# The column copies of a token mix: three engines share what GpSimd did for the most part

## The reference, cut to what matters

```
v = fno_layer(tokens_norm, value_w, value_skip_w, value_skip_b, (H, W))
dprod = softmax(einsum('bhtd,bhsd->bhts', qf, kf) / scale)
attn = einsum('bhts,bhsd->bhtd', dprod, vf)
attn = fno_layer(attn, proj_w, proj_skip_w, proj_skip_b, (H, W))
attn = instance_norm(attn + tokens, attn_norm_g, attn_norm_b)
m = instance_norm(attn, norm2_g, norm2_b)
m = fno_layer(m, mixer_w1, ..., norm=(mixer_norm_g1, mixer_norm_b1), act=gelu)
```

## Time and profile before

| | |
|---|---|
| median of 3 runs | 540.05 us (538.45 to 540.66) |
| profiled execution | 538.36 us |
| its span | 536.6 us |
| TensorE busy, matmuls | 378.2 us (70%) |
| VectorE busy | 380.9 us (71%) |
| ScalarE busy | 264.1 us (49%) |
| GpSimd busy | 280.3 us (52%) |
| GpSimd's column copies, L587 | 24, 30.1 us, 1296 ns each |

### The profile page before, as it was taken

How to read it: one execution, slowest core, us unless ns; L and a number is a source line. 1 busy time by engine, 2 the same in 40 slices (tenths; PEclk the granted TensorE clock), 3 DMA queues, 4 the chain that set the end, 5 groups by cost and what they waited for, 6 DMA issues and landing times.

```text
span 536.6 us, 8617 instructions
## 1 busy us (share of the span) xinstructions
PE 378.2 (70%) x3153; PEld 294.4 (55%) x3153; DVE 380.9 (71%) x982; ACT 264.1 (49%) x523; POOL 280.3 (52%) x294
## 2 busy tenths in 40 slices
PE   0489999974556699999994094766566556799590
PEld 0488996944111599988983083433333225466490
DVE  4999424264957776279997948677777656999791
ACT  1467742330210387346550131688888976599000
POOL 0587998300002496899898156766666069700000
PEclk9998999788687799779997587599999996899796
DMA  8969970499920200001665000000000000000299
GB/s 234 291 159 247 285 206 1 98 220 256 421 112 0 60 2 2 0 1 55 183 174 160 1 0 1 0 1 2 0 2 0 1 1 0 1 0 1 76 285 267
DMA packets 61082, 51.03 MB, mean 95 GB/s; under 512 B 4896, under 2 KB 54480, under 8 KB 60016
## 3 DMA queue, kind: packets, MB, share of 16 engines
q1 hardware_dynamic: 61040, 50.48, 33.4%
HBM read 30.45 MB, written 16.88 MB: 88 GB/s over the span
## 4 chain that ended last, share of the span: by engine, by line
DVE 41%; PE 25%; POOL 13%; ACT 6%; issue 5%; DMA 4%; SPq 3%; DVEq 0%
PE PS L628 23%; DVE PS L1430 7%; DVE BIG L1226 5%; DVE SML L1128 5%; POOL BIG L614 3%; DVE BIG L1398 3%; POOL BIG L545 3%; DMA BIG<-BIG 3%; POOL BIG L609 2%; PE PS L632 2%; DVE SML L1412 2%; DVE BIG L1315 2%; DVE BIG L1481 2%; SPq L502 2%; POOL BIG L561 2%
## 5 line engine op out<-in xcount | busy, mean ns | idle before, releaser
L628 PE MATMUL PS<-CST,BIG 128*128 128x122 f32 (+7 forms) x996 | 134.0, 330 | 30.8 <-POOL BIG L545 22.3
L628 PEld LDWEIGHTS PS<-CST,BIG 128*128 128x128 f32 (+1 forms) x996 | 119.1, 208 | 48.6 <-issue 36.0
L632 PE MATMUL PS<-CST,BIG 128*128 128x128 f32 (+1 forms) x326 | 53.7, 312 | 73.2 <-ACT SML L382 26.8
L632 PEld LDWEIGHTS PS<-CST,BIG 128*128 128x128 f32 (+1 forms) x326 | 43.4, 188 | 94.8 <-issue 59.9
L628 PE MATMUL PS<-BIG 128*32 128x32 f32 (+2 forms) x1216 | 67.7, 391 | 18.0 <-DVE BIG L1226 13.7
L587 POOL COPY BIG<-BIG 128x512 f32<-128x512 f32 x24 | 30.1, 1296 | 80.5 <-DVE BIG L1226 72.4
L628 PEld LDWEIGHTS PS<-BIG 128*32 128x32 f32 (+1 forms) x1216 | 50.8, 229 | 33.7 <-issue 17.1
L1128 DVE BATCH_NORM_STATS2 SML<-BIG 128x6 f32<-128x128 f32 x256 | 58.8, 301 | 9.1 <-DMA BIG<-in_x 7.8
L609 POOL TENSOR_TENSOR BIG<-BIG,SML 128x512 f32<-128x512 f32 x32 | 33.3, 1041 | 47.2 <-DVE SML L1150 30.5
L545 POOL TENSOR_SCALAR BIG<-BIG,SML 128x128 f32<-128x128 f32 x72 | 44.0, 676 | 24.5 <-DVE SML L1150 24.5
L628 PE MATMUL PS<-BIG,SML 128*128 128x256 f32 (+3 forms) x214 | 49.8, 471 | 5.8 <-ACT BIG L1076 5.8
(11 more groups left out here) (207 smaller groups left out, 588.7 us busy)
## 6 DMA issues: line engine op xcount, KB each, us to landing
xn_rows<-BIG SPq DMA_DIRECT2D x8, 1024.0 KB, 9.5
BIG<-xn_rows SPq DMA_DIRECT2D x8, 1024.0 KB, 23.9
BIG<-in_x SPq DMA_DIRECT2D x32, 256.0 KB, 2.9
out_x<-BIG SPq DMA_DIRECT2D x32, 256.0 KB, 3.7
BIG<-wy_rows SPq DMA_DIRECT2D x16, 192.0 KB, 6.2
BIG<-BIG SPq DMA_DIRECT2D x16, 192.0 KB, 11.5
BIG<-in_L_conv_mixer_w SPq DMA_DIRECT2D x2, 544.0 KB, 6.1
CST<-in_const SPq DMA_DIRECT2D x1, 579.5 KB, 8.9
```

The source lines that it names most:

```text
L628: return pe.matmul(o, l, rhs, start=start, stop=stop, **k)
L632: return pe.matmul(o, i, ident[0:n, 0:n], is_transpose=True, start=True, stop=True)
```

## The change

GpSimd keeps the even groups. VectorE takes groups 1, 5, 9, ..., 29 and ScalarE keeps 3, 7, ..., 31. VectorE's copies stand at four places of its block: group 1 ahead of the wait for `p_ma`, group 5 after L1284, groups 9 and 13 after L1287, groups 17, 21, 25 and 29 after L1297. There is one new semaphore, `x_mix_dve`.

```
             for g in range(32):
-                if g % MIX_ACT != MIX_ACT - 1:
+                if g % 2 == 0:
                     if g >= MIX_RING:
                         pool.wait_ge(S("mix_filled"), g + 1 - MIX_RING)
...
-                if g % MIX_ACT == MIX_ACT - 1:
-                    pe.wait_ge(S("x_mix_act"), (g + 1) // MIX_ACT)
+                if g % 2 == 0:
+                    pe.wait_ge(S("x_mix_pool"), g // 2 + 1)
                 else:
-                    pe.wait_ge(S("x_mix_pool"), g + 1 - (g + 1) // MIX_ACT)
+                    pe.wait_ge(S("x_mix_act" if g % 4 == 3 else "x_mix_dve"), g // 4 + 1)
...
+            def mix_columns(*groups):
+
+                for g in groups:
+                    if g >= MIX_RING:
+                        dve.wait_ge(S("mix_filled"), g + 1 - MIX_RING)
+                    dve.tensor_copy(x_mix[:, g % MIX_RING], columns(g)).then_inc(S("x_mix_dve"), 1)
...
             dve.wait_ge(S("ma"), 1)
 
+            dve.wait_ge(S("xt_in"), 16 * XC)
+            mix_columns(1)
             dve.wait_ge(S("p_ma"), 1)
...
             link(TS(y_m, y_m, s("al"), None, ALU.mult))
+            mix_columns(5)
             dve.wait_ge(S("kap_filled"), 1)
             dve.tensor_copy(kap, PS[:, 3, 0:NT]).then_inc(S("kap"), 1)
             link(TT(s("x0"), s("sm"), s("sm"), ALU.mult))
+            mix_columns(9, 13)
             dve.wait_ge(S("p_z1"), 1)
...
             TS(z3_1[:, :, 0, :], z3_1[:, :, 2, :], -1.0, None, ALU.mult).then_inc(S("z3_1"), 1)
+            mix_columns(17, 21, 25, 29)
```

## The result

The changed kernel takes 544.39 us (median of 6 runs, 541.33 to 548.77) against 538.32 (median of 6, 533.78 to 540.66): **1.0168 times the kernel before, 95% interval 1.0121 to 1.0215**. All ratios here are those on record, taken over the fast executions of both kernels; they are not the quotient of the two medians, which is 1.0113 in this case. In a second series the ratio was 1.0125 (1.0079 to 1.0172). The kernel is slower, as forecast, and its time is inside the range. The profiled execution, 548.77 us with a span of 547.0, is the slowest of its six.

A forecast was written before the change was run, and what follows sets the result against it. TensorE was taken to bound the mix, not the copies. Standstills of 2.7 and 3.3 us less 0.6 regained make 5.4, with 1.7 for the clock 7.1; on the median of 540.05 this gives 547.1 us, range 542.4 to 551.

The forecast's parts named there:

- The two late copies: VectorE's copies of groups 5 and 17 come late in the mix; TensorE stands still 2.7 and 3.3 us.
- The sum: For the mix: standstills 2.7 and 3.3, less 0.6 regained, 5.4 us; with 1.7 for the clock, 7.1.
- The third term: Standstill before group 17: its copy comes 6.0 us after group 13's end, TensorE wants it after 2.7; 3.3 us.
- The one fall: TensorE's clock halves after the second standstill, 3.4 us of work losing 1.7 us; ends 0 and 3.4.
- The copy's price: One VectorE column copy, every element read with a stride, takes 0.65 us; ends 0.43 and 1.1.
- The copy of group 1: VectorE's copy ahead of the wait for p_ma delays the start by some 0.1 us; ends 0 to 0.6.
- The meetings: GpSimd's copies of 6 and 8 hold up VectorE before group 5, that of 20 before 17; 1.0 us each.
- Group 11: Its 0.6 us lateness, from ScalarE's late copy, is regained if zw comes before ScalarE needs it.
- Group 9's copy follows at once, 3 us ahead of its use: VectorE's copy of group 9, right behind that of 5, was to be in time by 3 us.
- TensorE bounds this stage, not the copies: In the token mix GpSimd's 24 copies arrive in time, up to five groups ahead; TensorE sets the pace.
- The relief of the lock: Rival: fewer GpSimd copies free VectorE's chain, group 11's gap closes, nothing new is late; 539.4 us; 6%.
- The row of GpSimd operations that would starve a VectorE copy: Rival: each late VectorE copy loses another 1 us behind GpSimd's, both standstills cost clock; 10.8 us more, 550.9; 14%.

The follow-up runs named there:

- e6: The changed kernel run again without edits, in a second series; 1.0125 times the kernel before, profiled mix 40.89 us.
- e1: Changed kernel with only VectorE's copy of group 17 moved early, between the request for root r1 and its taking; 1.0087 times the kernel before.
- e2: Changed kernel with only VectorE's copy of group 5 moved early, between the second and third products for zw; 1.0064 times the kernel before.
- e5: e3 with VectorE's copy of 9 also ahead of the y_m scaling and that of 21 ahead of the z3_1 addition; 1.0001 times the kernel before.
- e4: Changed kernel with the copies of groups 5 and 17 given back to GpSimd, which makes 18; 1.0039 times the kernel before.
- e3: Changed kernel with VectorE's copies of groups 5 and 17 both moved early; 1.0023 times the kernel before.
- e9: Kernel before the change, plus 14 matrix products of constants on TensorE ahead of its wait for the scaled identity; 1.0052 times the kernel before.
- e10: e5 plus 14 matrix products of constants on TensorE ahead of the mix; 1.0033 times the kernel before.
- e8: Changed kernel with GpSimd holding its copies of groups 8 and 20 until VectorE's of 5 and 17 are done; 1.0097 times the kernel before.

## Why the prediction was right

**The two late copies.** Right in place, order and cause. Forecast 2.7 and 3.3 us; measured idle 2.79 and 2.83 (2.49 and 2.85 in e6), and by the starts of groups 3.0 each. e1 and e2 take them away one by one, e5 both with what they had hidden.

**The sum.** Forecast 2.7 - 0.6 + 3.3 + 1.7 = 7.1 for the mix with one fall; measured 6.75. In the medians it is 6.1 us. The third term was 0.3 too large; most of it is L1294 (now L1305), which took 1.95 with its meeting where I had 1.2 + 1.0. The time forecast, 547.1 us, is 2.7 above the measured median of 544.39: 1.0 of it is the sum, and 1.7 is the median of the kernel before, 540.05 over three executions and 538.32 over six.

**The one fall.** Here luck helped. The fall was a choice between none and two; the profile of the changed kernel has one, of 1.70 us, and that of the same kernel in e6 none, with a mix 5.1 us longer than before against the 5.4 forecast without a fall. The medians' 6.1 lies between the two.

**The copy's price.** 0.65 taken, 0.73 to 0.75 measured, 0.80 right after a wait. That lies between L1374 (0.43) and L1277 (1.10), which fits a charge for the stride; no run here changes the stride alone. By the two results a cycle that the Trainium skill gives for a float32 copy within SBUF ("VectorE: DVE Perf Modes", section "Mode 2×_2P — use both read ports for one tensor") the copy would take the 0.43 of L1374, an estimate; the trace doesn't bear that out for this copy.

**The copy of group 1.** The request ends at 179.14 and ScalarE takes the root at 179.18, when its own copy is done too; from VectorE's L1266 (before: L1259) to the first group it is 5.64 us, 5.45 before. Forecast some 0.1, measured 0.2.

**The meetings.** Their number was right (two before group 5, one before 17) and their price near: 1.0 us each in the forecast, 0.8, 0.9 and 0.7 measured (L1290, L1291 and L1305 less what they take alone). Their partners were not. I had GpSimd's copy of 6 hold up L1280 (now L1289). In fact that copy was ready at 185.24, during L1288, and L1289 still went ahead of it in its own 1.15 us; the operations held up were L1290 and L1291. That didn't move the sum.

**Group 11** was regained, as forecast: no idle stands there. The changed kernel alone doesn't show the reason, since its standstill before group 5 gives ScalarE time as well; in e5, which has no such standstill, group 11 is in time too.

**What was wrong, though the sum didn't show it.** Two sentences hold only under a condition that the prediction doesn't name. "Group 9's copy follows at once, 3 us ahead of its use" and "Groups 21, 25 and 29 follow back to back or wait for a slot, in time" are true only while TensorE stands still before 5 and 17. e2 to e4 show 9 late by 1.3 to 2.3 us, and e1, e3 and e4 show 21 late by 0.2 to 1.0, once it doesn't. And "TensorE bounds this stage, not the copies" holds only at the clock of the earlier trace rows: e9 shows the copies binding once the first groups run at 1.00.

**The rivals.** The relief of the lock was real and small: `zw` came 8.3 us after the mix's start (189.69), not 10.0 (190.85). TensorE doesn't wait for `zw` itself, and the 0.7 us at group 11 is all that could come of it; the copies of 5 and 17 were late all the same. The row of GpSimd operations that would starve a VectorE copy did not occur; the longest copy of the changed kernel is 0.80 us, and those of e5 and e10, at most 1.57, were held up by one operation. The Trainium skill ("SBUF — State Buffer", section "Who interferes with whom") says that the engine that issues first has the shared ports for its whole instruction while the other is blocked. e8 agrees with it: with GpSimd's copy of 8 away, L1291's 1.54 us became 0.68.

What stays open: in which executions the clock falls behind a standstill. Of the timed executions only the mean clock is known, and one profile was taken of each kernel (two of the changed one). Open too is where most of e9's time goes.

## What to carry to other kernels

When work is shared out to an engine that runs in order, the question is not how busy it is but what stands ahead of each new piece, and when its user wants it. Go down the block with the user's due times: here four of eight copies stood behind work that did not need to come first, and moving them to idle stretches (ahead of the taking of a root) or between independent steps won back the loss: 1.0001 times the kernel before, to 0.3%. And after each repair look at the next user: a standstill covers every lateness behind it that is shorter.

## What the runs showed that was not expected

- A wait at one point made later copies timely. With the 2.8 us before group 5 gone, 1.3 to 2.3 us came back before group 9.
- Keeping TensorE busy ahead of the mix raised its clock as meant (3.84 us for 32 records, not 6.31), yet both kernels were slower, by 0.5% (0.3 to 0.8%) and 0.3% (0.1 to 0.6%). In the mix the copies were then late and the clock fell afterwards; that is as much as e10's loss, and 0.7 us of e9's 2.8.
- A GpSimd copy that is ready during one VectorE operation may have to let the next one pass as well: ready at 185.24 within L1288, it held up only L1290. In the kernel before, the first of GpSimd's copies that met VectorE's chain, at 182.95, let L1278 pass in 1.10 us, and only then did the two alternate.
